# A mixture-of-experts kernel on one core: 21 large and 29 small expert tiles in another order, ScalarE copies, tables from seven batches' counts

## What is computed

```
h = layernorm(x) * (1 + ca) + sa
x = x + ga * attention(h)                      # scores, tanh, exp, per batch 1024 x 1024
h = layernorm(x) * (1 + cb) + sb
logits = h @ Wg;  top 2 experts of each token; top_w = softmax(top 2)
sparse = sum over the 2 experts e of top_w * (relu(h @ W1[e] + b1[e]) @ W2[e] + b2[e])
shared = relu(h @ Ws1 + bs1) @ Ws2 + bs2       # D_FF = 512
x = x + gb * (sparse + shared)
```

## Time and profile before

| | |
|---|---|
| median of 3 runs | 655.79 us |
| the profiled execution | 649.55 us, span 647.8 us |
| TensorE busy | 612.4 us (95%) |
| VectorE, ScalarE, POOL busy | 454.9, 396.2, 339.2 us (70%, 61%, 52%) |
| mean granted clock | 0.982 |

### The profile page before, as it was taken

The page is one execution under the profiler, slowest core; times in us unless marked ns, Lnnn a source line. Parts: engine busy times, 40 slices in busy tenths (PEclk is TensorE's granted clock), DMA queues, the critical chain, the costliest instruction groups (busy, mean ns, idle before and its releaser), DMA issues.

```text
span 647.8 us, 12480 instructions
## 1 busy us (share of the span) xinstructions
PE 612.4 (95%) x4304; PEld 559.4 (86%) x4304; DVE 454.9 (70%) x1414; ACT 396.2 (61%) x631; POOL 339.2 (52%) x342
## 2 busy tenths in 40 slices
PE   4998999999999998987999999999999999999995
PEld 3787888898989897886998999999999999999995
DVE  6869797989898989886775564544545445453788
ACT  3786787878787876544345555565655656555441
POOL 3542605766666666677560575555655556556000
PEclk9998999999999999977999999999999999999998
DMA  7340000111101111111165456556666566601972
GB/s 251 145 162 2 1 1 18 34 33 34 39 30 39 34 34 38 37 43 45 64 198 201 153 175 202 187 178 202 192 212 192 181 200 191 203 31 35 359 307 113
DMA packets 32015, 77.67 MB, mean 120 GB/s; under 512 B 7183, under 2 KB 13359, under 8 KB 31825
## 3 DMA queue, kind: packets, MB, share of 16 engines
q1 hardware_dynamic: 22592, 59.48, 27.6%
q0 software_dynamic: 8640, 16.93, 7.7%
q10 hardware_dynamic: 720, 0.47, 0.2%
HBM read 54.52 MB, written 23.25 MB: 120 GB/s over the span
## 4 chain that ended last, share of the span: by engine, by line
PE 49%; DVE 3%; issue 1%; ACT 1%; ACTq 0%
PE value L1952 18%; PE misc L1952 7%; PE score L1748 7%; PE score L1750 7%; PE score L1749 7%; PE value L2003 2%; PE misc L1789 1%; PE value L2042 1%; DVE res L1661 0%; DVE rows_all L1172 0%; ACT work L986 0%; DVE rows_all L1660 0%; DVE rows_all L1659 0%; DVE rows_all L1657 0%; DVE h_t L1670 0%
## 5 line engine op out<-in xcount | busy, mean ns | idle before, releaser
L802 POOL DMA_INDIRECT rows_z<-tile_y,tags x138 | 139.2, 1009 | 115.0 <-DVE tile_y L1577 49.2
L1748 PE MATMUL score<-h_hi,h_lo 128*128 128x512 f32 (+1 forms) x252 | 94.2, 374 | 1.9 <-DVE h_hi L1286 1.8
L1776 PE MATMUL value<-w_ring,work 128*128 128x129 f32 x768 | 94.1, 280 | 1.0 <-ACT work L860 0.9
L1776 PEld LDWEIGHTS value<-w_ring,work 128*128 128x128 f32 x768 | 92.1, 196 | 3.3 <-ACT work L860 1.3
L986 ACT ACTIVATE work<-score,w_ring 128x512 f32<-128x512 f32 (+1 forms) x96 | 53.1, 615 | 60.6 <-PE score L1750 59.1
L1750 PE MATMUL score<-h_hi,h_lo 128*128 128x512 f32 (+1 forms) x252 | 89.3, 354 | 0.0
L1749 PE MATMUL score<-h_hi,h_lo 128*128 128x512 f32 (+1 forms) x252 | 89.0, 353 | 0.0
L606 POOL DMA_INDIRECT rows_x<-work,slot x64 | 65.0, 1016 | 40.2 <-issue 15.5
L858 ACT ACTIVATE work<-work 128x1024 f32<-128x1024 f32 x64 | 67.2, 1050 | 30.4 <-DVE work L1182 30.2
L1182 DVE TENSOR_TENSOR work<-score,lw 128x1024 f32<-128x1024 f32 x64 | 76.4, 1214 | 3.7 <-PE score L1750 3.2
L986 ACT ACTIVATE work<-score,w_shared 128x512 f32<-128x512 f32 x64 | 40.3, 684 | 52.5 <-PE score L1750 51.2
(11 more groups left out here) (255 smaller groups left out, 1257.1 us busy)
## 6 DMA issues: line engine op xcount, KB each, us to landing
w_ring<-packs SPq DMA_DIRECT2D x24, 578.0 KB, 3.8
rows_all<-packs SPq DMA_DIRECT2D x23, 578.0 KB, 3.9
lw<-rows_x SPq DMA_DIRECT2D x24, 260.0 KB, 3.8
res<-x SPq DMA_DIRECT2D x7, 512.0 KB, 7.7
h_t<-rows_z SPq DMA_DIRECT2D x3, 1024.0 KB, 10.6
mod<-mod_rows SPq DMA_DIRECT2D x1, 2560.0 KB, 8.6
rows_z<-tile_y,tags POOLq DMA_INDIRECT x142
rows_all<-rows_z SPq DMA_DIRECT2D x2, 1024.0 KB, 13.1
```

What stands on the lines that cost most here:

```text
L802: nc.gpsimd.indirect_dma_start(rows_z[:, :], bass.IndirectOffsetOnAxis(ap=tags[pos][:, k, 0:1].bitcast(I32), axis=0), tile_y[par][:, k, :] ...
L1748: nc.tensor.matmul(out, a_lo, b_hi, start=True, stop=False)
L1776: ins = nc.tensor.matmul(value[:, s // 3, c0:c0 + D + 1], prob[:, t % 4, s * P:(s + 1) * P], normal[b % 3][:, t, :], start=(t == 0 and s % ...
```

## The change

* `LARGE_TILES` goes from 24 to 21, so there are 29 small tiles and 50 in all; the rows stay 18176. The order is no longer large, small in turn: two large ones first, then `1 0` nineteen times (1 is small), with a second small tile behind ten of the pairs, so that ten times two small tiles stand side by side; the last four are small, large, small, large as before. Row buffers (`slot_of`) keep three for each size, weight buffers go by j modulo 6. Loads of rows wait for the tile that last had the buffer.
* The large tiles' table comes from the counts of batches 0 to 6. A new matmul `early_ranks` (after the carry of batch 6) and a new `early_counts` give them; `large_tiles` reads these and stands ahead of `total_counts`. What was its tail is now the head of `small_tiles`. SP loads the weights and rows of e0 and e1 once batches 0 to 6 are scattered; the pads, the weights of e2 and the wait for the last batch's scatter (`last_scattered`) come behind.
* ScalarE copies each front tile out of the accumulation (`front_copy`) into `h2_t`; VectorE does bias, gate and sum in `add_shared_front`, two tiles before the experts, one in the entry, five in the loop behind large tiles. `add_bias` moves behind later large tiles.
* The order ahead of the experts changes on TensorE, VectorE and ScalarE, as the diff shows; `ranks(B - 2)` now stands ahead of the last `values`. POOL's sends of the last two batches wait for no relu; `rstd_2(B - 1)` stands one send earlier. The entry into the loop has its own order for e0 and e1.

```diff
-LARGE_TILES = 24
+LARGE_TILES = 21
+FIRST_LARGE = 2
+def kinds():
+    groups, pairs = LARGE_TILES - FIRST_LARGE, SMALL_TILES - (LARGE_TILES - FIRST_LARGE)
+    kind = [0] * FIRST_LARGE
+    for i in range(groups):
+        twice = (i + 1) * pairs // (groups - 2) - i * pairs // (groups - 2) if i < groups - 2 else 0
+        kind += [1, 0] + [1] * twice
+    return kind
...  SP, ahead of the experts
+            sp.wait_ge(large_table_ready, 1)
+            for j in range(FIRST_LARGE):
+                load_weights(j)
+            for par in range(2):
+                sp.wait_ge(scattered[par], 16 * 2 * G * (B // 2 - par))
+            for j in range(FIRST_LARGE):
+                load_rows(j)
             sp.wait_ge(counted, 1)
...  pads
             sp.wait_ge(table_ready, 1)
+            for j in range(FIRST_LARGE, RING):
+                load_weights(j)
             sp.wait_ge(padded, 16 * (E + 1))
+            sp.wait_ge(last_scattered, 16 * 2 * G)
+            load_rows(FIRST_LARGE)
...  POOL
+            for _ in range(2 * G - 3 * (G - FIRST) + G // 2):
+                send_next()
             rstd_2(B - 1)
-            pool.wait_ge(hidden_ready, 5)
-            pool.wait_ge(hidden_ready, 9)
-            pool.wait_ge(hidden_ready, 12)
+            for _ in range(2 * G - G // 2 + 2 * G):
+                send_next()
...  ScalarE, ahead of the experts
+            def front_copy(n):
+                act.wait_ge(down_ready, n + 1)
+                nc.scalar.activation(front_y[n], yacc[n % 2], ACT.Copy).then_inc(y_evac, 1)
             relu(1, w_shared, 1)
+            split_x(3, 1, shared_rows(3))
+            front_copy(0)
+            relu(2, w_shared, 0)
+            split_x(4, 0, shared_rows(4))
+            front_copy(1)
+            relu(3, w_shared, 1)
             stage_h2t(B - 1, 0)
             stage_h2t(B - 1, 1, xt_ps)
+            split_x(5, 1, shared_rows(5))
+            front_copy(2)
             gap_exponent(B - 1)
+            relu(4, w_shared, 0)
...  VectorE, ahead of the experts (new order)
             count_chosen(B - 2, route_chain[B - 2])
             split_w(0, 0, w_shared)
+            split_x(0, 0, shared_rows(0))
+            split_x(1, 1, shared_rows(1))
             attend(B - 1)
+            take_ranks(B - 2)
+            assign(B - 2)
             scale_attended(B - 1)
+            split_x(2, 0, shared_rows(2))
             add_attended(B - 1)
             moments_2(B - 1)
+            split_x(3, 1, shared_rows(3))
+            early_counts()
             normalise_2(B - 1, last_xhat)
+            split_x(4, 0, shared_rows(4))
             last_rows()
             route_chain[B - 1] = choose(B - 1)
             count_chosen(B - 1, route_chain[B - 1])
+            split_x(5, 1, shared_rows(5))
             take_ranks(B - 1)
             assign(B - 1)
+            split_x(6, 0, shared_rows(6))
+            large_tiles()
             total_counts()
+            split_x(7, 1, shared_rows(7))
             small_tiles()
             small_table()
-            shared(4) ... shared(6)
+            add_shared_front(0)
+            add_shared_front(1)
...  TensorE, ahead of the experts (new order)
             values(B - 1, 1, G - 2)
+            ranks(B - 2)
             values(B - 1, 1, G - 1)
+            shared_up(0)
+            shared_up(1)
             pe.wait_ge(value_used, B)
             shared_down(0)
+            early_ranks()
             shared_up(2)
+            shared_down(1)
+            shared_up(3)
+            pe.wait_ge(early_counted, 1)
             transpose_h2(B - 1, 0, misc, last_xhat)
             transpose_h2(B - 1, 1, xt_ps, last_xhat)
+            shared_down(2)
             gate_logits(B - 1)
             shared_up(4)
             shared_down(3)
+            ranks(B - 1)
             shared_up(5)
+            total_ranks()
             shared_down(4)
...
+            transpose_rows(0)
             shared_down(FRONT - 1)
+            transpose_rows(1)
+            expert_up(0)
+            expert_up(1)
+            expert_down(0)
+            transpose_rows(2)
+            expert_down(1)
+            transpose_rows(3)
+            expert_up(2)
+            transpose_rows(4)
+            for j in range(2, ROW_TILES - 3):
+                expert(j)
```

More of the change, by code:

```diff
@@ L1028, in expert_x @@
-            def expert_x(i, pos):
-                act.wait_ge(xt_ps_ready, CYCLE * i + pos + 1)
-                split_x(FRONT + CYCLE * i + pos, pos % 2, xt_ps[:, 0:rows_of(pos)])
-            def expert_relu(i, pos):
-                relu(FRONT + CYCLE * i + pos, w_exp[pos], pos % RING, rows_of(pos))
-            def expert(i, pos):
-                expert_relu(*ahead(i, pos, 1))
-                expert_w(*ahead(i, pos, 3))
-                expert_x(*ahead(i, pos, 3))
-            expert_w(0, 0)
@@ new lines, in expert_x, with expert_relu, expert @@
+            def expert_x(j):
+                act.wait_ge(xt_ps_ready, j + 1)
+                split_x(FRONT + j, j % 2, xt_ps[:, 0:rows_of(j)])
+            def expert_relu(j):
+                relu(FRONT + j, w_exp[j % SLOTS], j % RING, rows_of(j))
+            def expert(j):
+                expert_relu(j + 1)
+                expert_w(j + 3)
+                expert_x(j + 3)
+            expert_w(0)
+            front_copy(6)
+            expert_x(0)
+            expert_w(1)
+            front_copy(7)
@@ L1497, in large_tiles, with small_tiles @@
                 dve.wait_ge(large_table_ready, 1)
+            def small_tiles():
+                ends = sums[:, 0, 3, :]
                 tables(nc.vector.tensor_tensor(rest[:, :], ends[:, own], ends[:, before_], ALU.subtract))
@@ L1962, in shared_down, with early_ranks @@
                 down(n, w_shared, n % 2, first=(n < 2))
+            def early_ranks():
+                pe.wait_ge(carried, B - 1)
+                nc.tensor.matmul(misc[:, 0:E], ones[:, :], carry[:, :], start=True, stop=True).then_inc(early_total_ready, 1)
             def total_ranks():
@@ L1996, in _ @@
             pe.wait_ge(counted, 1)
-            def transpose_rows(i, pos, first=False):
-                pe.wait_ge(x_loaded[pos], loads(i))
-                if not first:
-                    pe.wait_ge(x_split, FRONT + CYCLE * i + pos)
-                for k in range(rows_of(pos) // P):
-                    ins = nc.tensor.transpose(xt_ps[:, k * P:(k + 1) * P], tile_x[pos][:, k, 0:D], ident[:, :])
-                ins.then_inc(xt_ps_ready, 1)
-            def expert_up(i, pos):
-                j = CYCLE * i + pos
-                up(FRONT + j, 1 + j, pos % 2, (pos + 1) % 2, rows_of(pos))
@@ L2026, in _, with transpose_rows @@
-            for pos in range(CYCLE - 4):
-                expert(CYCLES - 1, pos)
-            for pos in range(CYCLE - 4, CYCLE - 2):
-                expert_up(CYCLES - 1, pos + 1)
-                expert_down(CYCLES - 1, pos)
+            def transpose_rows(j):
+                pe.wait_ge(x_loaded[slot_of(j)], loads(j))
+                if j > 0:
+                    pe.wait_ge(x_split, FRONT + j)
+                for k in range(rows_of(j) // P):
+                    ins = nc.tensor.transpose(xt_ps[:, k * P:(k + 1) * P], tile_x[slot_of(j)][:, k, 0:D], ident[:, :])
+                ins.then_inc(xt_ps_ready, 1)
```

405 lines of the change are left out of this document (171 added, 234 removed).

## The result

| | changed kernel, us | before beside it, us | ratio, 95% interval |
|---|---|---|---|
| first measurement | 674.03 (668.65 to 679.88, 6 runs) | 655.00 (653.47 to 657.45) | 1.0266 [1.0234, 1.0298] |
| second (e4) | 639.39 (638.88 to 640.08) | 649.82 (648.55 to 650.99) | 0.9853 [0.9837, 0.9869] |
| third (e5) | 639.18 (639.01 to 639.49) | 649.46 (648.77 to 650.49) | 0.9840 [0.9824, 0.9856] |
| fourth (e8) | 639.61 (638.71 to 640.04) | 649.81 (649.04 to 649.89) | 0.9845 [0.9830, 0.9860] |
| fifth (e12) | 639.54 (638.69 to 640.25) | 649.69 (648.82 to 650.40) | 0.9843 [0.9826, 0.9859] |

The forecast was 645.1 us. The first measurement is 19.0 us slower than before, on the side that the forecast gave 5%. The five later ones ran on five different chips, and are 10.2 to 10.4 us faster than before, where the forecast's sum had 10.7.

A forecast was written before the change was run, and what follows sets the result against it. TensorE's own work bounds the expert loop; ahead of it TensorE loses time to idle waits and half clock. Gains 10.2 (front) + 0.8 (entry) - 0.3 (loop) = 10.7 us, off 655.8: 645.1 us; range 642.5 to 650.

The forecast's parts named there:

- the 6.2 us between the two: Whole kernel: difference between the profiled 649.55 us and the median 655.79, taken as equal before and after the change.
- waits that I have not seen: Catch-all case for the whole kernel, chance 0.06: 0.01 still faster, 0.04 no difference, 0.01 slower.
- Start of the front: TensorE ahead of up(0): 1.4 us idle for ranks(B - 2), then half clock, up(0) at 282.7, 0.5 us later than before.
- the one listed first: Rival, start of the front: clock comes back despite the gap, up(0) at 280.9, 1.8 us more gained, 643.3 us; chance 0.22.
- The last batch: Front: VectorE's moments end at 293.4, normalised rows at 298.1, 3 us before TensorE's transposes need them, so no wait.
- Up to the first expert up: Front, from up(0): 10.8 us of losses go, first expert up at 337.6 instead of 347.8, gain 10.2 us.
- third rival: Chain ahead of the front longer: transposes wait 2 us, clock falls for 3.5 us (1.7), 3.7 in all, 648.8 us; chance 0.13.
- ScalarE's copies at nothing: Front: eight ScalarE copies of front tiles, 5.2 us in all, fit its idle time and cost TensorE nothing.
- Entry: Entry into the experts: two waits of 1.24 us give way to one of about 0.4; gain 0.8 us.
- Last batch's rows: Entry: rows of e2 (an expert tile) issued at 338.8, landed at 342.0, needed at 346.8; margin 4.8 us.
- The second rival: Last batch's rows 9 us later through slow sends; TensorE waits 4 us, then half clock (1.7): 650.8 us; chance 0.10.
- Loop: Expert loop: six small tiles for three large cost 0.3 us; no idle time, weights keep 3.2 us margin behind two small tiles.

The follow-up runs named there:

- e4: The changed kernel unchanged, second measurement, on another place: 639.39 us, ratio 0.9853 to the kernel before.
- e5: The changed kernel unchanged, third measurement, on another chip: 639.18 us, ratio 0.9840 to the kernel before.
- e8: The changed kernel unchanged, fourth measurement, on another chip: 639.61 us, ratio 0.9845 to the kernel before.
- e12: The changed kernel unchanged, fifth measurement, base for the others on that chip: 639.54 us, ratio 0.9843 to the kernel before.
- e10: The changed kernel with ranks(B - 2) put back behind the last values: 636.81 us, ratio 0.9803 to the kernel before.
- e3: The kernel before with its three waits of POOL for relu halves taken out of the last batch's sends: 649.49 us, ratio 0.9998.
- e13: The changed kernel with TensorE's two transposes of the last batch ahead of down(1) and up(3), so that TensorE waits: 643.24 us, ratio 0.9906 to the kernel before.
- e14: The changed kernel with ScalarE making each of its eight front-tile copies twice: 640.64 us, ratio 0.9862 to the kernel before.
- e16: The changed kernel unchanged, sixth measurement, on another chip: 639.47 us, ratio 0.9847 to the kernel before.
- e11: The changed kernel with 60 more DMAs of 32 KB, issued by SP once ranks(B - 2) is used: 639.73 us, ratio 0.9848 to the kernel before.
- e15: The changed kernel with 12 more DRAM-to-DRAM copies (578 KB each) issued by SP ahead of the large tiles' weights: 640.49 us, ratio 0.9862 to the kernel before.
- e2: The changed kernel with GpSimd's sends paced by waits in the front and the expert loop: 639.92 us, ratio 0.9850 to the kernel before.
- e1: The changed kernel with only the front's sends (last two batches) cut into groups by waits for relu halves: 639.69 us, ratio 0.9858 to the kernel before.
- e6: The same kernel as e2 (all sends paced), on the third place: 639.48 us, ratio 0.9842 to the kernel before.
- e7: The same kernel as e1 (only the front's sends paced), on the third place: 640.18 us, ratio 0.9853 to the kernel before.
- e9: The same kernel as e2 (all sends paced), on the fourth place: 639.83 us, ratio 0.9845 to the kernel before.
- e17: The same kernel as e2 (all sends paced), on the sixth place: 639.72 us, ratio 0.9862 to the kernel before.

## Why the prediction was wrong, and what of it was right

**The step that failed** is the first one: "the 6.2 us between the two I take as the same on both sides, since nothing in the trace shows them". The profiled run of `before` had 649.55 us, the median beside it 655.79. On five other chips `before` took 648.55 to 650.99 us in each of its runs. So 649.55 is the kernel, and 655.79 is the kernel with something on top that belongs to where or when it ran. The forecast added it as a constant. It isn't one: it was 5.3 us for `before` (655.0 - 649.7) and 34.5 for the changed kernel (674.0 - 639.5). What makes up the 34.5 is in the first measurement's profile, and its cause stays open (below). The two numbers stood 1% apart, and the three runs behind the median agreed within 0.4% (654.22 to 656.35); that was on the table before the prediction, and should have been carried as a case of its own. In the forecast's list, "waits that I have not seen" had 0.01 for slower.

**The steps inside the kernel**, by the undisturbed profile e4, whose base is the same as that of the trace of before:

- *Start of the front.* Forecast: 1.4 us idle, half clock, `up(0)` at 282.7. Measured: 0.95 idle, granted clock 0.52 up to 282.6, `up(0)` at 282.56. The sum is right, partly by luck: the idle time was shorter, and the ranks behind it, at half clock, longer (0.88 from 278.42 to 279.30, where the forecast had 0.5). The reason given for the half clock is not borne out: in e8 it was low already ahead of the gap, e10 without the gap has it low too, but back 2 us earlier, and in e3 a gap of 1.95 us left it at 1.00. The sentence "1.85 us of idle time were enough" reads as a cause what was one run's sequence. (The rival that this paragraph calls the second is the one listed first, with 643.3.)
- *The last batch.* Moments 293.4 forecast and 293.4 measured (292.73 + 0.64), rows 298.1 and 298.0 (295.85 + 2.17), transposes without a wait. Right.
- *Up to the first expert up.* Forecast 337.6, gain 10.2; measured 337.94, gain 9.9 (347.84 - 337.94).
- *The cost of a late chain* (third rival). A wait of 2 us was priced at 3.7, with 1.7 for the clock. e13 puts 2.5 us there; its span is 2.9 longer and its median 3.7, and in the profiled run the clock stays. So the term for the clock did not come there; the length of the gap alone doesn't tell.
- *ScalarE's copies at nothing*: borne out by e14, to within its 1.1 us.
- *Entry.* Forecast 0.4 of waiting, gain 0.8; measured 0.21, gain 1.0.
- *Last batch's rows.* The rows of expert tile 2 (the forecast's e2) were to be issued at 338.8. GpSimd's last send ended at 338.6, 1.3 late, and SP waited 4.1 us for it to land, so it issued them at 342.82, 4.2 us behind the send's end where the forecast had 1.5. (The pads took 9.0 us and not 8.0, but were over by 337, so they cost nothing here.) The rows had landed by 344.86 (their 16 landing records), 2.0 us after the issue and not 3.2, and TensorE took them at 347.42 with no wait: a margin of 2.6 us where the forecast had 4.8. The second rival was nearer than the forecast had it.
- *Loop.* No idle time, no late weights. `last_up` starts at 571.56 instead of 581.86: 10.3 us gained in all, where the sum had 10.7.

Built on 649.55, the same sum would have given 638.9 us; five chips measured 639.2 to 639.6.

**What the first measurement was** is not settled. Shown, in its one profile: TensorE's matmuls came 0.84 us apart instead of 0.23 in the worst stretch, ScalarE and VectorE started 2.4 to 2.5 us behind their inputs, and SP's pads took 12.4 us instead of 9.0, all with no releaser in the program that would explain it; every unbroken row of seven and more sends in the loop ended in a stall, and most rows of five did not; about half of the landing records are missing from the first sends on. Neither the rows of sends (e4, e5, e8, e12, e16), nor 60 small DMAs beside them (e11), nor full DMA engines (e15) bring the stalls about elsewhere. Not shown: that the sends have to do with it. That would take a kernel with short rows throughout, beside this one, in a place where `before` takes 655 us; e2 is not such a kernel, as its loop keeps rows of eight and ten, and none of the five chips was such a place. The theory that fits is that the place slows something which long rows of sends use up, so that a kernel with shorter ones loses 5 us and this one 34; it is argued, not tested. A rival that fits as well, and is as untested: what lost the records of the sends also held up the engines, so that the stalls belong to the recording of that measurement. Against the theory: `before` has 9 and 11 sends in a row in its own front, and its trace has no such idle time; but that trace comes from an undisturbed run.

## What to carry to other kernels

When the profiled run and the median beside it differ by more than the runs scatter, the difference is a case with a chance of its own, not a constant on both sides: forecast against the undisturbed number, and say what the other would do. Putting independent tiles ahead of work that waits for a slow chain pays what the trace says, 10 us here; but something moved up to be early (the ranks of batch 6) is worth a sum of its own, as it cost 2.3 to 2.8 us of idle time and low clock for rows that nobody waited for. Pacing GpSimd's sends in the front cost nothing measurable here (e1, e2, e6, e7, e9, e17: within 1.0 us of the unpaced kernel), but no run shows that it helps. An edit that is meant to break a pattern is checked in its own trace first: e2's waits were there, and its rows of sends as long as before. And where an engine waits for nothing, count whether the profile has all its records before reading a cause out of the names.

## What the runs showed of the hardware

- The same program took 639.2 to 639.6 us on five chips and 674.0 in the first measurement, and `before` 649.5 to 649.8 and 655.0. A ratio against a kernel measured beside it doesn't take such a difference out.
- In that first measurement, and in no other profile, engines went on late with nothing to wait for: matmuls of 512 columns 0.84 us apart instead of 0.23 (TensorE, 340 to 349 us), 2.5 us from input to start (ScalarE, 287.99), 2.4 us (VectorE, 286.48), 12.4 us instead of 9.0 for eight pads (SP). GpSimd's sends kept their 1.26 us. The same profile lacks about half of its landing records (3133 instead of 6320 after 100 us). The cause is open.
- At a granted clock of 0.50 matmuls of 512 columns start 0.43 us apart (317.61 to 318.04 in the first measurement), at 1.00 0.23 us.
- The clock and short gaps: 2.53 us without work at full clock left the granted clock at 1.00 (e13), and so did 1.95 us (e3), while after 1.85 us the kernel before had 0.55, and after 3.38 us 0.51. The Trainium skill, "TensorE: Matmul & The Clock Gate", section "HAM oscillation — how this bites in real kernels", ties the fall to long idle gaps; e13, e3 and the 3.38 us agree, the 0.55 after 1.85 us doesn't. Of gaps of 1 to 3 us these rows give no rule.
- TensorE doesn't notice DMA engines that are busy to 0.99 at 322 GB/s (e15): 76 matmuls in 10 us, as without.
- GpSimd's indirect sends in an unbroken row start 1.26 us apart in the front and 1.29 in the loop (0.96 to 0.98 busy, 0.30 between); a few take 1.4 to 2.2 us. 60 small DMAs of 32 KB from SP's queue take 0.52 us each to issue (31.21 us, e11).
